# The latent scores with their low products on 64 rows each, behind both high products

## The reference

```
q      = (x @ W_q), 16 heads of 128
latent = x @ W_kv_down                      # 64 features
kv     = (latent @ W_kv_up), 16 heads of 128
scores = q . kv / sqrt(128)
out    = softmax(scores) @ kv, then @ W_o
```

## Time and profile before

| | |
|---|---|
| median of 3 runs | 1670.85 us (1670.62 to 1672.13) |
| profiled execution | 1665.35 us |
| its span, first to last instruction | 1663.6 us |
| mean granted TensorE clock | 0.934 of full speed |
| latent attention, about | 1124 to 1518 us of the span |

### The profile page before, as it was taken

The page is one execution under the profiler, slowest core; times in us unless marked ns, Lnnn a source line. Parts: engine busy times, 40 slices in busy tenths (PEclk is TensorE's granted clock), DMA queues, the critical chain, the costliest instruction groups (busy, mean ns, idle before and its releaser), DMA issues. The chain is left out here.

```text
span 1663.6 us, 39494 instructions
## 1 busy us (share of the span) xinstructions
PE 1424.6 (86%) x14334; PEld 984.3 (59%) x14334; DVE 1074.0 (65%) x2743; ACT 756.4 (45%) x1786; POOL 775.7 (47%) x741
## 2 busy tenths in 40 slices
PE   6879996647898996888999377878999999997898
PEld 3556664424555554455666256645667777676687
DVE  6862222577775654783222488958898888874888
ACT  5434443345556533553444212127776666662322
POOL 4554333754410000454333566508998888982000
PEclk9999998679899997989999689989999999999899
DMA  9309995421100002513998232200000000000000
GB/s 270 100 10 267 310 323 175 148 73 48 51 17 1 1 1 70 160 34 106 295 319 266 77 87 80 76 1 14 4 17 3 16 4 3 16 4 3 13 19 20
DMA packets 92664, 145.50 MB, mean 87 GB/s; under 512 B 25032, under 2 KB 52528, under 8 KB 92512
## 3 DMA queue, kind: packets, MB, share of 16 engines
q1 hardware_dynamic: 62816, 93.06, 18.9%
q0 software_dynamic: 15360, 37.77, 7.6%
q10 hardware_dynamic: 14336, 12.59, 2.7%
HBM read 122.39 MB, written 18.87 MB: 85 GB/s over the span
## 5 line engine op out<-in xcount | busy, mean ns | idle before, releaser
L2299 POOL TENSOR_TENSOR sb_m_prob<-sb_m_prob,sb_m_rinv 128x512 f32<-128x512 f32 x256 | 260.4, 1043 | 44.1 <-DVE sb_m_rinv L2349 40.4
L1273 POOL DMA_INDIRECT sb_c_rows<-slot_rows,sb_slot x192 | 193.4, 1007 | 97.9 <-issue 52.1
L2229 ACT ACTIVATE sb_m_prob<-m_ps_s,sb_m_nmax 128x512 f32<-128x512 f32 x256 | 173.8, 683 | 125.1 <-DVE sb_m_nmax L2355 124.4
L1106 POOL DMA_INDIRECT e_xn<-xn_rows,sb_table x128 | 118.0, 922 | 180.1 <-PE e_ps_x L1185 167.6
L1256 DVE TENSOR_TENSOR sb_e_h<-sb_e_sg,e_ps_gu 96x176 f32<-96x176 f32 x128 | 42.6, 333 | 226.9 <-ACT sb_e_sg L1232 226.9
L2355 DVE TENSOR_REDUCE sb_m_nmax<-m_ps_s 128x1 f32<-128x512 f32 x256 | 163.9, 682 | 29.4 <-PE m_ps_s L2133 26.9
L1194 PE MATMUL e_ps_gu<-e_wgu,sb_e_xT 128*96 128x352 f32 x512 | 172.8, 459 | 0.5 <-ACT sb_e_xT L1226 0.5
L2363 DVE STREAM_TRANSPOSE sb_m_pT<-sb_m_prob 128x1024 f32<-128x1024 f32 x128 | 157.6, 1232 | 0.0
L2146 PE MATMUL m_ps_v<-sb_m_pT,sb_m_lat_rows 32*64 32x128 f32 x8192 | 135.2, 273 | 5.6 <-issue 4.8
L2132 PE MATMUL m_ps_s<-sb_m_latT_high,sb_m_qa 128*128 128x512 f32 x256 | 125.6, 490 | 15.4 <-ACT sb_m_prob L2229 15.3
L2146 PEld LDWEIGHTS m_ps_v<-sb_m_pT,sb_m_lat_rows 32*64 32x64 f32 x8192 | 119.0, 130 | 29.1 <-issue 28.1
(11 more groups left out here) (280 smaller groups left out, 3072.4 us busy)
## 6 DMA issues: line engine op xcount, KB each, us to landing
e_wgu<-wgu SPq DMA_DIRECT2D x128, 352.0 KB, 6.7
e_wdn<-wdn SPq DMA_DIRECT2D x128, 192.0 KB, 6.8
slot_rows<-sb_e_y ACTq DMA_DIRECT2D x128, 96.0 KB, 6.1
xn_rows<-e_xn SPq DMA_DIRECT2D x16, 256.0 KB, 2.2
sb_c_rows<-slot_rows,sb_slot POOLq DMA_INDIRECT x192, 2.8
sb_x<-x SPq DMA_DIRECT2D x4, 512.0 KB, 5.3
e_xn<-xn_rows,sb_table POOLq DMA_INDIRECT x128, 6.4
sb_g_zm<-wqT SPq DMA_DIRECT2D x1, 2048.0 KB, 9.0
```

The lines of the kernel that those rows point to most:

```text
L1106: pool.indirect_dma_start(x, None, k.xn_rows[:, :], bass.IndirectOffsetOnAxis(ap=k.table[:, e:e + 1], axis=0))\
L1273: pool.indirect_dma_start(rows[u][j][:, :], None, k.slot_rows[:, :], bass.IndirectOffsetOnAxis(ap=k.slot[:, n, j:j + 1], axis=0))\
L2229: act.activation(prob[s % 4][:, hh, :], ps_s[j % 3][:, :], ACT.Exp, bias=nmax[s % 2][:, hh:hh + 1], accum_out=rsum[s % 2][:, hh:hh + 1]).t ...
L2299: pool.tensor_tensor(part, part, rinv[s % 2][:, hh:hh + 1].to_broadcast([P, T]), ALU.mult)\
```

## The change

Both heads' high products are issued first, and then both heads' low products. The low product no longer runs over all 128 rows but over the 64 rows in which the query's high part of that head lies: rows 0 to 63 for head 0, rows 64 to 127 for head 1. The product of the query's low part with the latent's low part is thereby no longer formed. The wait for a free bank stays ahead of each high product, and each low product still counts up `s_ready`.

```diff
--- before.py
+++ after.py
@@ -2125,12 +2125,16 @@
                     pe.wait_ge(q_ready, 2 * (pair + 1))
                     evicted(pe, ("latT", b))
                 cols = slice(t * P, (t + 1) * P)
+                high, low = latT[b % 2]
                 for hh in range(2):
                     j = 2 * s + hh
                     if j >= 3:
                         pe.wait_ge(p_ready, j - 2)
-                    pe.matmul(ps_s[j % 3][:, :], q[:, hh, cols], latT[b % 2][0][:, :], start=True, stop=False)
-                    pe.matmul(ps_s[j % 3][:, :], q[:, hh, cols], latT[b % 2][1][:, :], start=False, stop=True).then_inc(s_ready, 1)
+                    pe.matmul(ps_s[j % 3][:, :], q[:, hh, cols], high[:, :], start=True, stop=False)
+                for hh in range(2):
+                    j = 2 * s + hh
+                    pe.matmul(ps_s[j % 3][:, :], q[rows_of(hh), hh, cols], low[rows_of(hh), :],
+                              start=False, stop=True).then_inc(s_ready, 1)
 
             def values(pair, half):
                 b, of = pair // PAIRS, pT[pair % 2]
```

## The result

The changed kernel takes 1702.51 us, median of 4 runs (1696.91 to 1706.46), against 1670.73 us for the kernel before (4 runs). The ratio is 1.018 (95% interval 1.016 to 1.021), and by it the change costs 30 us. I had forecast 1690 within 1658 to 1704, slower. So the direction is right and the time lies inside the range, by 1.5 us, but the kernel lost 30 us where my sum had 19.

The account below looks back on a forecast made before the run. TensorE was taken to bound the latent attention, with head 0's score critical at 19 waits. Waits +12.5, full blocks +7.6 and values -0.9 made +19.2 us on 1670.85, hence 1690 us, range 1658 to 1704.

Parts of the forecast that it names:

- Pairing: Latent scores: both 64-row low products run together in 0.23 us, saving one product of 0.23 us a step.
- The switch in rows: Between 128-row and 64-row products: 0.10 us drain plus 0.11 us exposed weight load, 0.21 us each way.
- The rival of a free switch: Low loads slip in under high 1, a step is 0.23 us shorter; 1660 us, or 1655; chance 0.18.
- Head 0's score: In each step, complete 0.44 us later; its maximum at 1.21 us behind the step's start instead of 0.77.
- the path behind the release: At the 19 waits, from head 1's release to the values' load: 0.88 us instead of 0.66.
- the later score is covered everywhere else: Outside the 19 waits, head 0's later score costs nothing; tightest where queries follow, with 0.4 us of cover.
- The sum: Latent attention: waits +12.5, full blocks +7.6, values behind scores -0.9 us; together +19.2 us.
- The steady pairs: Pairs of heads: without a mix from 10.81 to about 11.6 us, with one from 13.3 to 13.6.
- the 19 waits: Steps where head 1 waits for head 0's exponential: 19 x (0.44 + 0.22) = +12.5 us.
- The eight full blocks that I left out: Of 48 full blocks behind scores, those at the start and batch changes, unpriced; the other 40 cost 0.19 us each.
- The granted clock: Latent attention stage read at full granted clock; no term or rival for a fall.

Follow-up runs that it names:

- rows_only: Changed kernel with the low products still on 64 rows but in the old order (high 0, low 0, high 1, low 1): 1742.34 us, ratio 1.0445.
- order_only: Changed kernel with the new order kept but the low products back on all 128 rows: 1683.68 us, ratio 1.0048.
- filler: Changed kernel with head 0's high product made four times more, discarded, in the 19 steps that wait: 1685.74 us, ratio 1.0074; repeated, 1685.22 us.
- at_waits: Changed kernel with new order and rows only in the 19 waiting steps and those just ahead, old form elsewhere: 1692.41 us, ratio 1.0128.
- but_waits: Changed kernel with the old form in the 19 waiting steps and those just ahead, new form elsewhere: 1680.24 us, ratio 1.0052.
- second profile: Changed kernel without further edit, run again beside the kernel before: 1696.28 us median, ratio 1.0150; the profile is of a 1706.8 us run.

## Why the prediction came out as it did

**Pairing.** Right. Two lows take the time of one (0.49 us), and cost 0.23 us more when both are in the same half.

**The switch in rows.** Right, and it was the open price: no row of before showed it. Into the lows 0.33 us from high 1, out of them 0.43 from load to load; rows_only repeats the turn four times a step at 0.43. The rival of a free switch is out: by it the lows would load 0.23 us or less behind high 1, and the changed kernel would have been faster. The Trainium skill, "TensorEngine Tiling (Array Packing)", Key Properties, says that changing the tiling mode drains the engine; these rows agree for a change in rows alone, 0.33 us where products of one shape are 0.23 apart.

**Head 0's score.** Right: 1.19 us against my 1.21. So was the path behind the release, 0.86 against 0.88. order_only shows what comes from the order alone, 8.2 us. That the later score is covered everywhere else was wrong in three steps (29, 61 and 93), which grew by 0.69 us where I had 0.19.

**The sum.** Mis-sized, by a little. With the clock held up (filler) the stage grew by 15.6 us, where I had 19.2. The steady pairs grew by 0.75 and 0.29 us, where 0.66 + 0.19 - 0.02 and 0.19 x 2 - 0.02 x 2 give 0.83 and 0.34. The term that was too large is the 19 waits. I had priced all of them as waits with values behind them, but only 14 are (so the values elsewhere are 50 blocks and not 45, which changes the sum by 0.1). Six of the 19 lie in the first nine steps, where all but one have no values behind them; by the starts of the high products, the first twelve steps took 29.6 us before and 31.2 in filler, 1.6 us for six waits that I had at 4. The later 13 cost 0.63 each, step ahead included, near my 0.66. The eight full blocks that I left out were not free: in filler's profile nearly all blocks cost 0.15 to 0.17 us each, at the batch changes too, so that a price somewhat too high and a count too low balanced. The rest is single waits that stand in one profile and not in the other.

**The granted clock.** Missed, and it is the larger error. The prediction read the stage as at full clock and took every price there; no term and no rival let the clock fall. In the changed kernel it does, in the first part of the stage and again late, where the steps that wait are close together. A step at half clock:

```profile
1147.39 0.80 PE L2133 MATMUL m_ps_s<-sb_m_latT_high,sb_m_qa 128*128 128x512 f32 x1 [0.87 <-ACT sb_m_prob L2233]
...
1148.12 0.80 PE L2136 MATMUL m_ps_s<-sb_m_latT_low,sb_m_qa 64*128 64x512 f32 x2
...
1148.84 3.78 PE L2110 MATMUL m_bank<-sb_m_xT,sb_absorb 128*128 128x512 f32 x4
```

High 1 behind its wait takes 0.80 us instead of 0.50, the lows 0.80 instead of 0.50, and the queries 3.78 instead of 1.88. These products fall where TensorE has just waited, and so the next score is later still. If filler's stage is taken as that of the full clock, the fall is worth 10.4 us in the first profile (408.7 - 398.3) and 18 in the second (416.3 - 398.3). These two figures are estimates, and the second is from the slowest of eight runs. at_waits and but_waits place the fall at the steps that wait and those just ahead of them, and filler, which adds only discarded products on 128 rows there, removes it. The runs do not name one cause beyond that. Longer waits alone don't do it to this extent: order_only waits 24.0 us in 22 places and its clock falls once. Long waits are not needed either: rows_only waits 1.9 us in all and has 0.89 in its first 62 us. 64-row products between steps that don't wait don't do it (but_waits, 1.00). What the changed kernel and rows_only share is 64-row products, with their switches, in the first nine steps, where TensorE is ahead of the exponentials. The Trainium skill, "TensorE: Matmul & The Clock Gate", Part 1, says that the throttled state is the default and activity releases it; filler agrees, with 1.00 where the changed kernel had 0.82. Half clock here is 1.2 GHz, the full one 2.4.

15.6 us for switches and order and 10 to 18 for the clock make 26 to 34 in the two profiles; the two ratios give 30 us (26 to 35) and 25 us (20 to 31). The measured time lies inside my range although I had no term for the clock. The range was wide enough on its slow side for other reasons, so it is luck that it holds.

The 9 us by which the first profile is late at its first score do not look like the change's. The stretch ahead of it (900 to 1124) has a clock of 0.82 there and of 0.87 before:

```profile
900.00:1124.00 224.00, 161.78 (x683) 118.97 (x681) 156.68 (x518) 53.21 (x159) 105.47 (x104) 0.87 0.24 70
```

The changed kernel's second profile reaches its first score at 1128.4, and other kernels here, with the same instructions up to there, anywhere between 1123.9 (but_waits) and 1135.9 (filler). What decides it from run to run was not settled.

Nothing that was tried beats the kernel before.

## What to carry to other kernels

Two half-height products that run together save the time of one product, 0.23 us. But going into the smaller tiles costs about as much (0.20 us), and so does coming out. By these figures, an estimate that no run here tests, pairing pays only where several pairs follow each other without a switch between them.

When an order is changed, ask which result is ready later and what waits for it with no slack: here head 0's score is ready 0.44 us later, because head 1's high product and a switch now stand ahead of its low one, and behind the wait for a bank there are three products where there were two.

TensorE's clock can be part of the price of a change. Where its products come less densely than before, by waits or by switches, look at the granted clock of that stretch, and try cheap throw-away products in the gap: if the time falls, the clock was part of the loss.

## What was not expected of the hardware

Four discarded products in each of 19 gaps, 76 x 0.23 = 17 us of added work for TensorE, made the changed kernel 11 us faster, and with them the granted clock of its first 55 us went from about 0.82 to 1.00. Gaps as long had little such effect where the lows still used all rows (order_only, 0.97 in its first 55 us), and with hardly a gap, but a switch at every product, the clock was 0.89 (rows_only). What exactly lets it fall, the runs leave open.
